# Moving routed rows in bursts, with nine kinds of segments and ones products in the routing

## The reference

```
gates = jax.nn.softmax(xt @ gate_w, axis=-1)
top_v, top_i = jax.lax.top_k(gates, K)                      # K = 2 of 8
top_v = top_v / jnp.sum(top_v, axis=-1, keepdims=True)
h = jax.nn.gelu(jnp.einsum('nd,edf->enf', xt, fc_w), approximate=False)
eo = jnp.einsum('enf,efd->end', h, proj_w)
sel = jnp.take_along_axis(jnp.swapaxes(eo, 0, 1), top_i[:, :, None], axis=1)
out = jnp.sum(sel * top_v[:, :, None], axis=1)
```

## Time and profile before

| | us |
|---|---|
| median of three runs (lowest, highest) | 612.52 (612.04, 613.9) |
| profiled execution, its own time | 612.42 |
| its span in the trace | 610.2 |
| TensorE busy | 532.3 (87%) |
| VectorE busy | 408.0 (67%) |
| GpSimd busy | 273.1 (45%) |
| ScalarE busy | 240.0 (39%) |

### The profile page before, as it was taken

The page is one execution under the profiler, slowest core; times in us unless marked ns, Lnnn a source line. Parts: engine busy times, 40 slices in busy tenths (PEclk is TensorE's granted clock), DMA queues, the critical chain, the costliest instruction groups (busy, mean ns, idle before and its releaser), DMA issues.

```text
span 610.2 us, 12226 instructions
## 1 busy us (share of the span) xinstructions
PE 532.3 (87%) x3768; PEld 457.4 (75%) x3769; DVE 408.0 (67%) x1452; ACT 240.0 (39%) x551; POOL 273.1 (45%) x505
## 2 busy tenths in 40 slices
PE   4999990699998699999999978999995499999992
PEld 2678750699997499888987856766784189999992
DVE  8888852233447995466678868878787765655573
ACT  3455510355554444434443223355550043333330
POOL 3464378666657306910000010445625768774332
PEclk9999855599999899989998989999996599999997
DMA  9998012122252300000000350002100132211234
GB/s 293 378 329 262 17 53 66 49 71 69 70 141 97 106 1 1 2 0 1 1 2 0 119 158 1 2 1 91 50 0 19 57 71 64 65 56 53 78 108 122
DMA packets 48152, 47.65 MB, mean 78 GB/s; under 512 B 6470, under 2 KB 37603, under 8 KB 47942
## 3 DMA queue, kind: packets, MB, share of 16 engines
q1 hardware_dynamic: 43558, 37.68, 21.0%
q0 software_dynamic: 4544, 9.38, 4.7%
HBM read 27.53 MB, written 19.51 MB: 77 GB/s over the span
## 4 chain that ended last, share of the span: by engine, by line
PE 73%; DVE 18%; issue 3%; another core or an unknown queue 3%; ACT 1%; DMA 1%; DVEq 0%; POOL 0%; POOLq 0%; SPq 0%; ACTq 0%
PE bank L2396 16%; PE bank L2407 10%; PE bank L1981 8%; PE bank L2177 4%; PE bank L2222 4%; PE bank L2261 4%; PE bank L2250 2%; PE bank L1970 2%; PE bank L1971 2%; PE bank L1972 2%; PE bank L2384 1%; PE bank L2319 1%; DVE stats L1101 1%; PE bank L2212 1%
## 5 line engine op out<-in xcount | busy, mean ns | idle before, releaser
L2396 PE MATMUL bank<-xT,wcur 128*128 128x128 f32 x936 | 120.6, 280 | 3.9 <-ACT xT L883 3.7
L2396 PEld LDWEIGHTS bank<-xT,wcur 128*128 128x128 f32 x936 | 113.6, 196 | 4.9 <-ACT xT L883 4.3
L691 POOL DMA_INDIRECT yt<-Y,dest_i x62 | 61.6, 994 | 57.8 <-ACT Y L899 34.7
L634 POOL TENSOR_SCALAR var_eps<-mv 128x4 f32<-128x4 f32 (+2 forms) x12 | 2.9, 238 | 184.6 <-DVEq L1807 97.4
L675 POOL DMA_INDIRECT xw<-XW,slot_i x64 | 63.2, 987 | 26.2 <-issue 16.3
L967 ACT ACTIVATE hT<-bank,b_cols 128x512 f32<-128x512 f32 x64 | 43.9, 688 | 63.7 <-PE bank L1972 63.2
L1434 DVE COPY wcur<-WA 128x512 f32 x78 | 38.1, 490 | 43.6 <-PE bank L2396 40.1
L1981 PE MATMUL bank<-WC,hT 128*128 128x128 f32 x512 | 64.8, 282 | 0.0
L1981 PEld LDWEIGHTS bank<-WC,hT 128*128 128x128 f32 x512 | 62.3, 197 | 1.4
L1577 DVE SCALAR_TENSOR_TENSOR X<-bank,G,X 128x128 f32<-128x128 f32 x128 | 36.0, 343 | 32.9 <-PE bank L1981 28.3
L1449 DVE TENSOR_TENSOR hT<-gb,bank 128x512 f32<-128x512 f32 x39 | 26.8, 687 | 40.1 <-ACT gb L888 36.9
(11 more groups left out here) (405 smaller groups left out, 1169.5 us busy)
## 6 DMA issues: line engine op xcount, KB each, us to landing
xw<-pad_rows SPq DMA_DIRECT2D x34, 260.0 KB, 4.6
xrow<-xw SPq DMA_DIRECT2D x78, 65.0 KB
WA<-in_fc_dram SPq DMA_DIRECT2D x16, 256.0 KB, 4.9
YT<-yt SPq DMA_DIRECT2D x16, 256.0 KB, 3.6
WA<-in_pj_dram SPq DMA_DIRECT2D x8, 256.0 KB, 5.6
WB<-in_fc_dram SPq DMA_DIRECT2D x8, 256.0 KB, 4.4
WB<-in_pj_dram SPq DMA_DIRECT2D x8, 256.0 KB, 6.2
X<-in_x_dram SPq DMA_DIRECT2D x2, 512.0 KB, 4.4
```

The costliest lines, as they stand in the source:

```text
L691: pool.indirect_dma_start(out=yt_dram, out_offset=bass.IndirectOffsetOnAxis(ap=dest_i[:, t:t + 1], axis=0), in_=y_slot(layer, t), in_offse ...
L2396: ins = pe.matmul(dst, wcur[:, s4, at:at + P], xT[s4 % 2][:, :], start=True, stop=True)
```

## The change

It has three parts. *Moves.* The scatters are cut into seven groups by `MOVED`, after 5, 6, 7, 8, 10, 12 and 16 tiles, and `BURSTS` names the groups before which GpSimd waits until the group ahead has landed. In the first mixture that gives 10 scatters, a wait, 6, a wait, 8, a wait, 8, with no pauses; in the last one 10, a wait, 4, the wait for `ex_xc`, 10 with pauses, and 8 between the first puts. SP waits for 5 tiles before the first load (10 scatters) and at slots 3, 5, 7, 9, 13 and 17 for the next groups. The segments go from 6 kinds to 9 (72 instead of 48), and the counts by which they are made from 2 to 4 per half. *TensorE's order in the routing.* In the first, V1 moves from before ranks(0) to behind the second logits, the row and values behind ranks(0), the keys ahead of the last `later_m`, and 33 ones products (10, 3, 6, 6 and 8) come in between; values use another bank. In the last, 44 ones products come in (16, 9, 9, 10), and the 14 before the first slot become 10. *VectorE.* The counts of the first half are made behind the scaling of the second; `values(1)`, `shares` and `split_row` go from ahead of the first slot into slots 1 to 6, and TensorE no longer waits for `values(1)` before its first slot. SP writes rows of the split (`ROWS_AT`) at slot 16 instead of 8. One cast of GpSimd at the start goes.

The diff, cut to its core:

```diff
-SOON = 6
...
+MOVED = (0, 5, 6, 7, 8, 10, 12, TILES)
+BURSTS = ((1, 4, 6), (1,))
+FILLED = [-(-(tiles * P * TOPK - PARTIAL) // P) for tiles in MOVED[1:-1]]
...
 FIRST_DONE = (GT * P * TOPK * 3 // 2 + PARTIAL) // P
-KINDS = 6
+KINDS = 9
...
+COUNTS = 4
+COUNTED = ((4, 1), (1, 2))
...
-WARM = 14
+WARM = 10
+LATER_VALUES = (2, 3, 4, 5)
...
+        def landed(layer, group):
+
+            def moves(groups):
+                return sum(TOPK * (MOVED[i + 1] - MOVED[i]) for i in groups if i % RING == group % RING)
+            return 16 * (layer * moves(range(len(MOVED) - 1)) + moves(range(group + 1)))
+
...
                     sp.wait_ge(dest_ready, base)
-                sp.wait_ge(scattered[0], 16 * TOPK * SOON * (layer + 1))
+                sp.wait_ge(scattered[0], landed(layer, 0))
                 for t in range(SLOTS):
-                    if t == SOON_ONLY:
-                        sp.wait_ge(scattered[1], 16 * TOPK * (GT - SOON) * (layer + 1))
-                    if t == FIRST_ONLY:
-                        sp.wait_ge(scattered[2], 16 * (MOVES // 2) * (layer + 1))
-                    if t == THREE_ONLY:
-                        sp.wait_ge(scattered[3], 16 * (MOVES // 2) * (layer + 1))
+                    if t in FILLED:
+                        group = FILLED.index(t) + 1
+                        sp.wait_ge(scattered[group % RING], landed(layer, group))
...
                 pool.wait_ge(routed, GROUPS * layer + 1)
-                for tile in range(GT):
+                last = len(MOVED) - 2
+                for tile in range(MOVED[1]):
                     for choice in range(TOPK):
-                        scatter(layer, 0 if tile < SOON else 1, tile, choice)
-                pool.wait_ge(scattered[0], 16 * TOPK * SOON * (layer + 1))
-                if layer == 0:
-                    pause()
-                else:
-                    pool.wait_ge(ex_xc, SLOTS + 1)
-                pool.wait_ge(routed, GROUPS * layer + 2)
-                for tile in range(GT, GT + GT // 2):
-                    for choice in range(TOPK):
-                        scatter(layer, 2, tile, choice)
-                        pause()
-                if layer == 0:
-                    for tile in range(GT + GT // 2, TILES):
+                        scatter(layer, 0, tile, choice)
+                for group in range(1, last + (layer == 0)):
+                    if group in BURSTS[layer]:
+                        pool.wait_ge(scattered[(group - 1) % RING], landed(layer, group - 1))
+                    if group >= RING:
+                        pool.wait_ge(scattered[group % RING], landed(layer, group - RING))
+                    if layer and group == RING - 1:
+                        pool.wait_ge(ex_xc, SLOTS + 1)
+                    for tile in range(MOVED[group], MOVED[group + 1]):
                         for choice in range(TOPK):
-                            scatter(layer, 3, tile, choice)
-                            pause()
+                            if layer and group >= RING - 1:
+                                pause()
+                            scatter(layer, group, tile, choice)
+                pool.wait_ge(scattered[last % RING], landed(layer, last - RING))
...
                     put(layer, t)
-                    if layer and t < GT // 2:
+                    if layer and t < TILES - MOVED[last]:
...
                             pause()
-                            scatter(layer, 3, GT + GT // 2 + t, choice)
+                            scatter(layer, last, MOVED[last] + t, choice)
...
                 choices(layer, g)
-                places(layer, g)
+                count = places(layer, g)
...
                     ln_scaled(half(1))
+                    first_counts(count)
...
                     weights(t)
-                if layer == 0:
-                    values(1)
-                shares(layer, 1)
...
                 done_counts(layer)
-                if layer == 0:
-                    split_row()
...
                         destinations(t + 1)
+                    if t == 1:
+                        shares(layer, 1)
+                    if layer == 0 and t in LATER_VALUES:
+                        values(1, [LATER_VALUES.index(t)])
+                    if layer == 0 and t == LATER_VALUES[-1] + 1:
+                        split_row()
...
                     later_context()
-                    later_row()
+                    warm(10, 6)
+                else:
+                    warm(16, 4)
...
                 if layer == 0:
-                    pe.wait_ge(dl_ready, 1)
+                    later_row()
                     values(1, wv3, range(GB))
+                    warm(3, 6)
+                else:
+                    warm(9, 4)
...
                 if layer == 0:
+                    later_values1()
                     later_m(0)
+                    warm(6, 7)
                     later_m(1)
+                else:
+                    warm(9, 4)
...
                 if layer == 0:
+                    pe.wait_ge(dl_ready, 2)
                     values(1, wv3, range(GB, B))
+                    warm(6, 7)
+                else:
+                    warm(10, 4)
...
                     later_m(2)
+                    later_keys()
+                    warm(8, 0)
                     later_m(3)
-                    later_keys()
...
                     pe.wait_ge(s1_evac, 8)
-                    pe.wait_ge(setup_evac, B + 3)
```

More of the change, by code:

```diff
@@ L83 @@
 YROUNDS = STEPS // YRING
-ROWS_AT = 2 * RING
+ROWS_AT = 4 * RING
 EPS = 1e-5
@@ L166, in build @@
         place_row = sb("place_row", [1, SLOTS], F32)
-        c68 = sb("c68", [P, 2, E], F32)
-        c8 = c68[:, 1, :]
+        c5678 = sb("c5678", [P, COUNTS, E], F32)
+        c8 = c5678[:, COUNTS - 1, :]
         home2 = sb("home2", [P, E], F32)
         ce8 = sb("ce8", [P, E], F32)
-        c1216 = sb("c1216", [P, 2, E], F32)
+        c10to16 = sb("c10to16", [P, COUNTS, E], F32)
         ends = sb("ends", [P, KINDS + 1, E], F32)
@@ L177, in build @@
         value = sb("value", [P, 2, SEGMENTS], F32)
+        expert_no = value[:, 1, :]
         tile_at = sb("tile_at", [1, SLOTS], I32)
@@ L426, in y_slot, with values_at @@
             return (Y if layer or t // YRING % 2 == 0 else YA)[:, t % YRING, :]
+        def landed(layer, group):
+            def moves(groups):
+                return sum(TOPK * (MOVED[i + 1] - MOVED[i]) for i in groups if i % RING == group % RING)
+            return 16 * (layer * moves(range(len(MOVED) - 1)) + moves(range(group + 1)))
+        def values_at(i, b):
+            at = (b + GB) % B if i else b
+            return bank[3 - i][:, at * P:(at + 1) * P]
         def turned_at(i):
@@ L673, in scatter @@
                 pool.wait_ge(const_ready, 3)
-                pool.wait_ge(routed, GROUPS * layer + (2 if group > 1 else 1))
+                pool.wait_ge(routed, GROUPS * layer + (2 if tile >= GT else 1))
                 pool.indirect_dma_start(
                     out=xw_dram, out_offset=bass.IndirectOffsetOnAxis(ap=slot_i[:, choice, tile:tile + 1], axis=0),
-                    in_=XW[:, tile, :], in_offset=None).then_inc(scattered[group], 16)
+                    in_=XW[:, tile, :], in_offset=None).then_inc(scattered[group % RING], 16)
             def put(layer, t):
@@ L743, in _ @@
             link(pool.iota(number_i[:, 0:SEGMENTS], [[0, KINDS], [1, E]], base=0, channel_multiplier=0))
-            pool.tensor_copy(value[:, 1, :], number_i[:, 0:SEGMENTS])
             link(pool.tensor_copy(expert_no[:, :], number_i[:, 0:SEGMENTS]))
@@ L851, in later_context, with later_values1 @@
                 ins.then_inc(s1_evac, 1)
+                act.wait_ge(r_mm, 1)
+                act.activation(rrow, bank[4][0:H, 2 * P:3 * P], ACT.Copy).then_inc(r_read, 1)
+            def later_values1():
                 act.wait_ge(s1_mm, 3)
                 act.activation(V1[:, :, :], bank[5][0:K, :].rearrange("p (b d) -> p b d", b=B), ACT.Copy).then_inc(s1_evac, 1)
-                act.wait_ge(r_mm, 1)
-                act.activation(rrow, bank[4][0:H, 2 * P:3 * P], ACT.Copy).then_inc(r_read, 1)
             def later_keys():
@@ L1183, in split_row, with values @@
                 split3([rparts[:, i, :] for i in range(PARTS)], rrow).then_inc(r_evac, 1)
-            def values(i):
+            def values(i, batches=range(B)):
                 dve.wait_ge(setup_mm, B + 5 if i else 3)
-                for b in range(B):
-                    v = bank[3 - 3 * i][:, b * P:(b + 1) * P].rearrange("p (c h d) -> p c h d", c=HC, h=HPC)
+                for b in batches:
+                    v = values_at(i, b).rearrange("p (c h d) -> p c h d", c=HC, h=HPC)
                     dve.tensor_tensor(VB[:, b, :, 0:HPC * DK].rearrange("p c (h d) -> p c h d", h=HPC), v,
@@ L1326, in places @@
                 rank = bank[2 * g + 1][:, 0:GT * E].rearrange("p (t e) -> p t e", e=E)
```

(7 more changed lines are left out.)

33 lines of the change are left out of this document (15 added, 18 removed).

## The result

The changed kernel takes 609.74 us at the median of 20 runs (607.3 to 613.14), the one before 613.12 beside it (20 runs, 609.68 to 615.99): a ratio of 0.995, interval 0.9932 to 0.9968. It is faster, by 3.4 us and not by the 25 that were forecast; the time lies outside the forecast's range (579 to 604). The profiled execution shown here took 611.43, span 609.3.

What follows compares the result with a forecast made beforehand. It took the first experts stage to be bound by its late start, all engines slowed by long scatter runs. From 612.4 us it subtracted 19.7 (layer 0) and 5.5 (last layer), giving 587; range 579 to 604.

Steps and rivals of the forecast that it cites:

- A long unbroken run of scatters brings the creeping on: Both layers' scatters around the first loads: slowing begins near a run's 12th scatter; the change keeps every run under 12.
- creeping: Around the first experts stage's start and in the last layer: all engines go on late, steps about 0.7 us, nothing visible behind.
- Rival 2: Onset in both layers: the run isn't the cause, the hole stays; 604 to 612 us, chance 0.10.
- A rest of some 3 us ends it, so each landing wait does: GpSimd between scatter groups: a landing of 2.36 us rests it enough to end the slowing; layer 0 gains 19.7 us.
- At the full clock ranks(1) at 81.9; I take T = 95: Layer 0 routing: full clock gives ranks(1) at 81.9, first up at 92.7; 2 us added for a half-clock piece.
- T: Start of layer 0's first up: 92.7 at full clock, 108 at half, taken as 95; 109.10 before.
- the half-clock sum: Layer 0 routing at half clock: logits end at 81.2, ranks(1) at 93.0, table passed at 97.6, first up at 108.
- Rival 1: Layer 0 routing: clock stays low up to the table; first up at 108, 7.2 gained, 600 us in all; chance 0.15.
- Slot 4 from T in 7.6 us: Layer 0's first slots: slot 4's up follows the first by four slots at 1.893 us, at 102.6 for 122.85.
- The puts' backlog: GpSimd in layer 0: puts begin at 119 with results waiting, last put at 173.7; VectorE's additions held 0 to 1 us.
- The last layer, 5.5 us: Last layer's first slot: load at 481.2, up at 484.4 for 489.92, so 5.5 us gained.
- Rival 3: Second `slot_i` of layer 0: rests of 2.4 us don't reset, clock low; 3 to 5 us longer, 616 us; chance 0.09.

Runs made afterwards that it cites:

- late_run: The kernel before with 15 pauses ahead of the first scatter of layer 0; ratio 1.0134.
- l1_pace: pace1 with a pause ahead of each of the last layer's first 14 scatters too; ratio 0.9871.
- rests: The changed kernel with four pauses behind each landing wait of layer 0, and a landing wait and four pauses ahead of the first put; ratio 1.0081.
- pace0: The changed kernel without its three landing waits in layer 0 and with no pauses ahead of its scatters; ratio 1.0002.
- pace1: The changed kernel without landing waits in layer 0, with one pause ahead of each scatter there; ratio 0.9884, 606.72 us.
- order_pace1: pace1 with TensorE's order of the kernel before and no ones products in the first routing; ratio 0.9833.
- pace2: The changed kernel without landing waits in layer 0, with two pauses ahead of each scatter there; ratio 1.0137.
- pace166: pace1 with pauses of 288 columns in place of 192 in layer 0; ratio 0.9875.

## Why the prediction was wrong

- **"A long unbroken run of scatters brings the creeping on": right as to the run.** late_run moved it with the run, and SP's moves of 0.7 us in the last layer went when it was paced (l1_pace: at most 51 ns). Rival 2's "same piece of program" was not the cause; that 609.74 lies in its band of 604 to 612 is luck. The Trainium skill ("DMA: Bandwidth & Descriptors", section "Issuing engines are not separate DMA queues") says that DMAs of all issuing engines run on the same 16 engines and interleave there. These engines' share was 0.21 to 0.31 from 95 to 130 in the traces shown, so by that alone spacing would win nothing. It won 1.1%: whatever is short, it is not these engines' time.
- **"A rest of some 3 us ends it, so each landing wait does": the step that failed.** The forecast set the creeping behind a rest at nothing, and so had layer 0 gain 19.7 us; its last up came 1.26 us later than before. The rests were 1.58, 3.10 and 1.89 us, and the creeping was back by the 6th scatter of the last burst (117.98). Making each rest at least 3.1 us (`rests`) won nothing, and behind 8.4 us (pace0) it was back by the 9th scatter. I had read two ends of creeping as its reset, though in both GpSimd had simply stopped sending. What counts is how closely the transfers follow each other: at 1.265 us large delays, at 1.52 small ones, at 2.05 none up to 163. The mean over the stage doesn't decide it, since `rests` and pace1 have the same (1.56 and 1.54).
- **"At the full clock ranks(1) at 81.9; I take T = 95": the size was off by 9 and 7.** The logits ended at 81.6, where the half-clock sum had 81.2; V1, 2.67 us ahead of ranks(0) before, took 4.5 behind the logits (81.54 to 86.05), the ones 2.43. Thus ranks(1) at 91.04. The step behind it was the clock: the ones were to bring the full one, and the granted clock was 0.64 from 70 to 80 and 0.51 from 80 to 90. Rival 1 was nearer on this stretch (93.0), not on T (108 for 102.43), since the granted clock was back at 1.00 from 90 to 95. The Trainium skill ("TensorE: Matmul & The Clock Gate", Part 1) says that activity releases the low clock. The trace does not agree here, with 10.00 of 10 us busy at 0.51. With the creeping paced away, the old order without ones had its first up 7 us before the new one at the same low clock (order_pace1 94.78, l1_pace 102.17), so in layer 0 order and ones cost time.
- **Slot 4 from T in 7.6 us:** 9.3, with waits for `wcur`. **Slot 10** was due at 102.6 + 6 x 1.893 = 114.0 and came at 135.48; of these 21.5 us 7.4 are T's, 1.7 the ramp's, 12.3 the second creeping.
- **The puts' backlog:** due from 119 to 174; it never formed, since results came no earlier. With the pace it did: in pace1 24 puts follow each other from 122.8 to 158.6. By 161 it was worked off, so it didn't set the end there either.
- **The last layer, 5.5 us:** 2.1. The creeping struck VectorE behind the table (the wait of 1.93 us ends at 483.52) with the 10 scatters and the rest of 1.60 just done, so a run under 12 is no safeguard. The ten ones behind it, which the forecast's sum leaves out, took 4.42 us at half clock and ended where the first transpose begins.
- **Rival 3** named the right place and mechanism (the second `slot_i` at 98, scatters that end at 121.5, creeping behind them), and the first stage did end later, by 1.3 us for the 3 to 5 it gave. Seven ups begun by 117 (three before) and the 2.1 us of the last layer kept the sum on the faster side.

## What to carry to other kernels

When every engine slows at once and nothing visible is late, look at how closely one engine's indirect transfers follow each other, and space them evenly before you split them into bursts. Two ends of a stall that coincide with a pause don't show that the pause resets it: test the pause by making it longer. Spacing has a price too: at 2.05 us a scatter the rows themselves came late (8.03 us in pace2), so pace no more than is needed.

## What the runs showed of the hardware

At one indirect transfer of 128 rows per 1.265 us, from about the 12th on (behind a rest sooner, from the 5th to the 9th on), engines that have nothing to do with them get results 2 to 10 us late, and some of SP's register moves take 0.70 us for 0.03. It is the same whether the transfers scatter rows (all runs) or put results (pace166, 6.02 us). The transfers themselves land as fast as ever (GpSimd's waits for a landing, 1.58 and 1.89 us in the changed kernel and 1.37 to 1.47 in `rests`, don't grow), and GpSimd keeps its step. Half the bytes change nothing. Which limit it is that they meet was not found. Each execution here has a recorded span, so no run tells whether it happens without the recording; until one does, the gain of pacing is shown for recorded executions alone. The Trainium skill ("NOTIFIC — the notification-queue block", section 7.1) says that the block that writes the records holds its producers back inside rather than lose one, which can stall an engine. That would fit engines that all wait for nothing visible, and no run here shows it.
